# A two-layer attention and feed-forward kernel on Trainium2: the timetable of state products, query turn, router, two down products and future-value products is changed

## What is computed

```
xn = layernorm(x)
x  = x + attn0(xn) + ffn0(xn)
xn = layernorm(x)
x  = x + attn1(xn) + moe(xn)

attn0: 16 heads of 8, rotary q and k, causal softmax with a bias;
       relu(probs + tau / row) @ v @ Wo   (relu(tau / row) also meets the masked, future tokens)
ffn0 : silu(xq @ Wg) * (xq @ Wu), both operands rounded to blocks of FP4, then @ Wd
attn1: linear attention, q and k = elu + 1, running state kv = sum of k (x) v,
       out = q @ kv / (q @ ks) @ Wout
moe  : router (softmax, best 2 of 4), y = sum over experts of comb_e * (silu(x Eg) * (x Eu)) @ Ed
       plus one shared expert
```

## Time and profile before

| what | us |
|---|---|
| median of 3 runs (lowest, highest) | 2108.49 (2107.59, 2109.04) |
| the profiled execution, its own time | 2108.19 |
| its span in the trace | 2106.2 |
| mean granted TensorE clock, share of full | 0.981 |
| busy PE, DVE, ACT, POOL | 1934.5, 1540.6, 1375.7, 1143.8 |

### The profile page before, as it was taken

How to read it: one execution, slowest core, us unless ns; L and a number is a source line. 1 busy time by engine, 2 the same in 40 slices (tenths; PEclk the granted TensorE clock), 3 DMA queues, 4 the chain that set the end, 5 groups by cost and what they waited for, 6 DMA issues and landing times.

```text
span 2106.2 us, 49813 instructions
## 1 busy us (share of the span) xinstructions
PE 1934.5 (92%) x17353; PEld 1264.0 (60%) x17353; DVE 1540.6 (73%) x5223; ACT 1375.7 (65%) x3861; POOL 1143.8 (54%) x1799
## 2 busy tenths in 40 slices
PE   3789999999999999999999999999999999998978
PEld 1455666656566575666657566575656657565645
DVE  6558778687776868778687877868777686876646
ACT  1677585675857667585766858567685766757531
POOL 4676374655637465473746647475563746545220
PEclk9779999999999999999999999999999999999999
DMA  5102021110301102020210201121030110201010
GB/s 146 27 9 44 4 39 23 34 29 8 54 4 38 24 20 42 4 56 6 39 24 18 44 4 39 23 39 24 10 52 4 38 24 17 40 4 34 4 32 6
DMA packets 172653, 59.37 MB, mean 28 GB/s; under 512 B 139643, under 2 KB 169971, under 8 KB 172403
## 3 DMA queue, kind: packets, MB, share of 16 engines
q1 hardware_dynamic: 172403, 56.19, 13.9%
HBM read 14.22 MB, written 4.19 MB: 9 GB/s over the span
## 4 chain that ended last, share of the span: by engine, by line
PE 56%; ACT 16%; DVE 12%; POOL 8%; issue 7%; DMA 1%; SPq 0%; ACTq 0%; DVEq 0%; POOLq 0%
PE ps L1124 11%; PE ps L1260 8%; PE ps L1195 8%; PE ps L1205 7%; ACT ring L946 5%; PE ps L1138 5%; PE ps L1114 4%; ACT pb L955 3%; PE ps L1245 3%; DVE ring L577 3%; PE ps L1183 2%; DVE lin L609 2%; POOL ring L843 2%; PE ps L1103 2%; PE ps L1171 2%
## 5 line engine op out<-in xcount | busy, mean ns | idle before, releaser
L843 POOL TENSOR_SCALAR ring<-ring,row_rcp,tau_row 128x128 f32<-128x128 f32 (+3 forms) x1024 | 625.5, 618 | 676.1 <-DVE row_rcp L584 676.1
L946 ACT ACTIVATE ring<-ring,neg_max 128x128 f32<-128x128 f32 (+3 forms) x1024 | 570.8, 558 | 504.0 <-DVE neg_max L577 499.4
L1124 PE MATMUL ps<-identf,ring 128*128 128x128 f32 x2560 | 378.6, 287 | 10.4 <-POOL ring L843 7.6
L955 ACT ACTIVATE pb<-ps 128x512 f32<-128x512 f32 x640 | 348.0, 583 | 27.5 <-PE ps L1124 23.2
L1124 PEld LDWEIGHTS ps<-identf,ring 128*128 128x128 f32 x2560 | 279.2, 143 | 83.4 <-issue 39.0
L577 DVE CUSTOM_DVE_ANT_1 ring<-ps,bias_t 128x384 f32<-128x384 f32 (+1 forms) x496 | 286.7, 614 | 53.7 <-PE ps L1114 46.4
L1260 PEld LDWEIGHTS ps<-ed_t,h 128*128 128x128 f32 (+1 forms) x1920 | 254.6, 191 | 97.2 <-issue 93.7
L1260 PE MATMUL ps<-ed_t,h 128*128 128x128 f32 (+1 forms) x1920 | 270.6, 277 | 0.0
L1205 PE MATMUL ps<-xn1T,eu_t 128*128 128x512 f32 (+1 forms) x480 | 256.5, 616 | 1.3 <-DVE h L633 1.2
L1195 PE MATMUL ps<-xn1T,eg_t 128*128 128x512 f32 (+1 forms) x480 | 255.6, 614 | 2.2 <-DVE h L626 2.1
L1114 PE MATMUL ps<-qkT 32*128 32x128 f16 (+3 forms) x1024 | 201.4, 308 | 47.1 <-DVE neg_max L577 28.0
(11 more groups left out here) (152 smaller groups left out, 2815.7 us busy)
## 6 DMA issues: line engine op xcount, KB each, us to landing
x_t<-x SPq DMA_DIRECT2D x16, 256.0 KB, 2.9
x<-x SPq DMA_DIRECT2D x16, 256.0 KB, 2.9
o_rows<-o_stack SPq DMA_DIRECT2D x256, 16.0 KB
out<-x SPq DMA_DIRECT2D x16, 256.0 KB, 2.3
qkT<-qkx SPq DMA_TRANSPOSE x128, 3.2
bias_t<-bias SPq DMA_DIRECT2D x1, 1536.0 KB, 7.8
eg_t<-eg SPq DMA_DIRECT2D x1, 860.0 KB
eu_t<-eu SPq DMA_DIRECT2D x1, 860.0 KB
```

The source lines that it names most:

```text
L843: pool.tensor_scalar(e, e, row_rcp[:, m % 2, r:r + 1], tau_row[:, i, HG * g + r:HG * g + r + 1], ALU.mult, ALU.add).then_inc(p_ok.sem, 1)
L946: act.activation(e, e, ACT.Exp, bias=neg_max[:, n % 2, r:r + 1], scale=-1.0, accum_out=row_sum[:, n % 2, r:r + 1]).then_inc(exp_ok.sem, 1)
L955: act.activation(pb[:, c % NPB, :], bank(turn_bank(q)), ACT.Relu).then_inc(t_taken[q % 2].sem, 1)
L1124: last = pe.transpose(o[:, r * P:(r + 1) * P], ring_of(i, r)[:, k * P:(k + 1) * P], idf)
```

## The change

Only places in the timetable are moved, and the sums get places of their own (`ADD_EXPERT`).

```
-TURN_H, FUTURE_V, FUTURE_Y = (ATT + 11, ATT + 13, ATT + 13, ATT + 15), ATT + 61, ATT + 63
+TURN_H, FUTURE_V, FUTURE_Y = (ATT + 11, ATT + 13, ATT + 13, ATT + 15), ATT + 67, ATT + 69
...
-KV, TURN_Q32 = (L1 + 29, L1 + 29, L1 + 31), L1 + 30
+KV, TURN_Q32 = (L1 + 33, L1 + 47, L1 + 53), L1 + 46
...
-ROUTER = L1 + 31
+ROUTER = L1 + 37
...
-DOWN1 = [GATE1[3 * e + 2] + 4 for e in range(NE - 1)] + [L1 + 65]
+DOWN1 = [L1 + p for p in (35, 44, 49, 56, 65)]
+ADD_EXPERT = [L1 + p for p in (43, 48, 53, 60, 69)]
...
-                    if p == DOWN1[e] + 4:
+                    if p == ADD_EXPERT[e]:
                         accumulate(b, e)
```

## The result

The changed kernel takes 2162.5 us (median of four runs, 2153.0 to 2169.0), the kernel before 2108.8 on the same chip: ratio 1.0252, 95% interval 1.0213 to 1.0291. It is slower, as forecast (2155, range 2131 to 2169). The sum behind the forecast is right in its places and signs. It counts 46.5 us for moved work and waits where 31 are measured, and it leaves out two costs that together come to some 23 us in the median run: the clock that Tensor loses behind the hole of slot 31, and the last frame. So the closeness of the total is in part luck.

A forecast was written before the change was run, and what follows sets the result against it. Tensor, busy 92%, was taken as the bound, with a hole in slots 28 to 32 held by other engines. Terms of 2.89 - 0.13 + 0.34 = 3.1 us a frame, times 15, added 46.5 to 2108.2: 2155, range 2131 to 2169.

The forecast's parts named there:

- floor of slot 32: First turn of probabilities in slot 32 waits for GpSimd's fourth scaled head, so removing 1.4 us of Tensor work gains 0.
- rival 3: Faster: removal around slots 28 to 32 pays because scaling doesn't hold slot 32; 2.2 us a frame gained, 2075; chance 0.05.
- if slot 32 comes earlier after slot 28 than before: Sign that the forecast is wrong, beside a fall in Tensor's idle time; no size given.
- none of these instructions comes behind one that is moved away: Slots 28 to 32: the tanh, silu, stacking and scaling Tensor waits for don't follow moved work, so gain 0.
- The two waits of slots 44 and 45: Second score product waits for Vector's `lin` masks, +0.4 us; up product's bank waits for Vector behind the first sum, +0.8.
- the wait of 0.25 that I gave Vector: Slots 48 and 49: Vector's second mask ends about 0.25 us after Tensor wants its bank, leaving -0.45 from -0.7.
- rival 2: Vector becomes the bound: rounding steps stay long (+0.95), router steps meet GpSimd's scaling (+0.3); 4.3 us a frame, 2173; chance 0.14.
- the forecast's own bounds: Slots 42 to 45: the two added waits for Vector, from 0.6 to 1.9 us a frame, 2146 to 2163.
- The end of the frame: Without `fy` at slot 63 Tensor arrives sooner, but GpSimd's last scaling holds the turn of probabilities: only -0.13 us.
- Frame 0 and the last frame, which has no attention, I take as unchanged: First and last frame: no change in time, so the sum counts only 15 frames.
- The hole stays (slots 28 to 32): Tensor's idle stretch, 1.32 us before the third state product, is no prize: removing 1.4 us of work there gains 0.
- Rival 1: Slots 42 to 49: Vector keeps up, only moved work counts; 1.65 us a frame, 25 in all, 2133; chance 0.22.

## Why the prediction was right, and where it wasn't

By its own steps, for a frame, in us:

| step | forecast | measured |
|---|---|---|
| slots 28 to 33: floor of slot 32, then a state product | 0 + 0.33 | +0.19 |
| slots 42 to 45: two tiles out, two waits in | -0.2 | -0.37 |
| slots 46, 47: turn, state product, two tiles | +2.18 | +1.98 |
| slots 48, 49: one tile out, the second sum in | -0.45 | -0.67 |
| slots 52, 53: a tile and a state product | +1.03 | +0.91 |
| end of frame and slots 0 to 7 | -0.13 + 0.34 | +0.08 |
| sum, with -0.04 in slot 36 | 3.1 | 2.08 |

**The floor of slot 32** held: the turn stands 9.60 us behind slot 28 and stood 9.66, and with one of its two supports taken away it didn't move (2.50 us of idling on GpSimd). It is rival 3 that falls here, in full: slot 31's hole grew by nearly the work that left it. Two sentences of the prediction don't hold, though. Its sign of being wrong, "if slot 32 comes earlier after slot 28 than before", came true by the letter (7.77 us for 8.72): it should have named the first turn of slot 32, not the slot's start. And "none of these instructions comes behind one that is moved away" is not so: Vector's silu stands behind the sum of slot 29's state products, which ends 0.3 us ahead of the tanh that silu waits for (both in the earlier trace rows). The sum's row in the trace of before:
```profile
1067.31 0.56 DVE L605 TENSOR_TENSOR state<-state,state_d 128x144 f32<-128x144 f32 x1
```
It cost the forecast nothing, since the tanh is later; it shows when the tanh is moved, as above.

**The two waits of slots 44 and 45** are there with their sizes, 0.38 and 0.82 against my 0.4 and 0.8. Slots 42 and 43 lose 1.57 us where I had 1.4 for the two tiles. The rows give the tiles 1.53, less 0.19 because the gate and up products now stand ahead of `lin` and scores and take 1.06 us each (0.96 and 0.97 before); the other 0.24 is a shorter wait of slot 42's own pair of scores (0.64 for 0.88), which I hadn't counted. In slots 46 and 47 the four moved groups take 2.17 for my 2.18, but the gate product of slot 47 now takes 0.86 us (1123.48 to 1124.34), between a state product and a tile, where it took 1.06 between `intra` and scores (1105.40 to 1106.46 before). That 0.2 is the difference to 1.98. What stands beside a group changes its price by 0.1 to 0.2 us.

**A state product** costs 0.24 to 0.25 us (1123.23 to 1123.48), not 0.33. The 0.33 was read in the hole, behind idling. Three of them are 0.25 us a frame too much in my sum.

**Slots 48 and 49**: the wait of 0.25 that I gave Vector never shows; the tile leaves 0.67 and that is all. The rounding steps are short (0.34 at 1127.66), as I took them, so rival 2 is out. Nor do the forecast's own bounds follow from its terms: 0 to 0.6 and 0 to 1.35 add up to 0 to 1.95 a frame, which is 2137 to 2166, and not to 0.6 to 1.9 and 2146 to 2163. The measured waits, 1.2, lie in either.

**The end of the frame**: the turn of the last probabilities stands 8.94 us after slot 62 and stood 9.04, -0.10 for my -0.13.

So the sum of the terms is 31 us for 15 frames and not 46.5. The execution that was profiled is 44.8 us longer than that of before, and this is where the rest is. The step **"Frame 0 and the last frame, which has no attention, I take as unchanged"** failed: frame 0 is 1.4 us shorter, as the future values of item 0 leave it, and from slot 63 of frame 15 to the end it is 104.2 us instead of 99.4, +4.8. The two stretches, before and after, each with one row of its product by `wo_t`:
```profile
2006.78:2106.20 99.42, 79.97 (x627) 52.35 (x626) 52.72 (x139) 25.68 (x56) 10.84 (x18) 0.95 0.09 20
...
2026.30 1.14 PE L1235 MATMUL ps<-wo_t,o_rows 128*128 128x128 f32 x8 [3.90 <-DMA o_rows<-o_stack]
```
```profile
2046.78:2151.00 104.22, 81.47 (x629) 52.78 (x628) 53.22 (x140) 25.63 (x56) 10.80 (x18) 0.93 0.09 19
...
2067.67 2.04 PE L1236 MATMUL ps<-wo_t,o_rows 128*128 128x128 f32 x8 [4.15 <-DMA o_rows<-o_stack]
...
2094.17 0.41 PE L1172 MATMUL ps<-qkT 32*128 32x128 f16 x8 [1.88 <-DMA qkT<-qkx]
```
With no attention beside it the second layer is a chain with Tensor idle a fifth of the time. The starts of its groups divide the 4.8 us. Up to the product by `wo_t` it is +1.4; item 15's future values, which left frame 15, now stand here. That product is shown as 2.04 us for 1.14, at the lower clock, and the next group is 0.9 later by it. From there to the first triangular products it is +0.1 only: they wait 1.88 us for the turned stack and waited 0.63 before, so here too the work that left made a wait longer and nothing earlier. From them to the first product by `sel_t` it is +2.4: the query turn and two state products take 1.0 us, and the shown waits for Vector grow from 1.4 to 3.1. Behind that nothing differs.

The sum so far, 31.2 - 1.4 + 4.8, leaves 10.2 us. Of these some 9 (6.0 and 2.8) are in stretches with the lower clock: frames 1 to 14 of the changed kernel exceed 126.95 by 10.0 together, those of before exceed 124.86 by 4.0, and frame 15, up to slot 63, exceeds the others by 2.8 more than before. The rest is a gain counted twice: the 1.2 us that slot 63 of frame 15 loses with `fy` are taken off in the 31.2 and again in the 4.8. The median run is 9.5 us longer still, at a clock of 0.965; no trace of it was kept, so that these too are clock is an inference from the mean.

The other step that failed is thus in the paragraph **"The hole stays (slots 28 to 32)"**: I costed the longer hole at nothing, because work that left an idle stretch can't delay anything. That is right for order and wrong for the clock. The trace of before had the sign, in frame 7, which takes 125.13 us, not 124.87. Around its slots 28 and 29:
```profile
936.60:940.00 3.40, 2.59 (x17) 1.88 (x18) 3.40 (x11) 3.40 (x11) 1.39 (x4) 0.77 0.11 22
```
I had read two frames at 1.00 and no other. The forecast came within 0.4% of the time by luck: two mistakes, 15 us too much and some 23 too little, went against each other. Rival 1 had 1.65 us a frame without the waits; with the prices measured that would be 0.9, and the waits are there, so it wasn't that either.

**What stays open**: why one frame gets the lower clock and the next, with the same rows, doesn't. The runs show how often, against the idle time, and no more. And from which waits of Vector the 1.7 us in the last frame come, row by row, I haven't shown.

## What to carry to other kernels

Work that fills a wait is free only where it stands; moved to a stretch in which the same engine is never idle, it costs its whole length, and the place it leaves stays as long as its next floor (here a tanh, Vector's own queue, a scaling and a DMA, one behind the other). Before removing work from a hole, list every floor at that height, and lift them together; before adding any, look for the waits that a product of 0.8 us would fill, since that gained 1.3% here with no new instruction. And count a longer hole on Tensor as a cost of its own: here the matmuls behind it ran at half clock in most frames.

## What the hardware showed that I hadn't expected

Where Tensor idled 2.46 us and then 0.83 more between groups of work, the granted clock fell to 1.2 GHz in most frames (0.52 over a stretch of 3.40 us). The frames that had it were longer by 0.3 to 2.3 us; the whole change lost 0.009 to 0.018 of mean clock by it (0.981 to 0.972 and 0.963). Useless turns of an identity, 2.2 us a frame, brought it back to 0.984 and saved 21 us; a third of them saved 10. With the same idle time divided otherwise (0.78 and 2.50 us) the lower clock stayed.

By the Trainium skill ("TensorE: Matmul & The Clock Gate", Part 1: The HAM clock gate) the array has two levels, 1.2 GHz idle or cold and 2.4 GHz busy. The rows agree on the levels (0.50 and 1.00 of the full clock) and on idling as the cause. They also show the lower level in work that follows a short idle time, in some frames and not in others, which the two levels alone don't tell.

A second finding: the same 128x144 state product takes 0.33 us to the next start behind an idle stretch (1069.62 to 1069.95) and 0.25 behind a busy one (1123.23 to 1123.48). Here a price read in a hole was too high for the place where the work went.
